# Splitting the first chunk's loads over two DMA queues, and storing the second chunk's rows earlier

## The reference, cut to what matters

```python
e = stack([tbl_f[ids[:, f]] for f in range(39)], axis=1)        # 2048 x 39 x 16
x0 = xk = e
for idx, (W, b) in enumerate([(w0, b0), (w1, b1), (w2, b2)]):
    z = relu(einsum('bhd,bkd,hks->bsd', x0, xk, W) + b[None, :, None])
    if idx != 2:
        xk = z[:, :64]          # feeds the next layer
        direct.append(z[:, 64:])
    else:
        direct.append(z)
logit = sum(concatenate(direct, axis=1), axis=-1)               # 2048 x 256
h = concatenate([logit, dense_ctx], axis=1)
y = relu(relu(h @ W_top1 + b_top1) @ W_top2 + b_top2) @ W_top3
```

## Time and profile before

| What | Number |
|---|---|
| Median of three runs | 2424.73 us |
| The profiled execution's own time | 2426.18 us |
| Its span (first to last instruction of the program) | 2424.2 us |
| TensorE (PE) busy | 2343.5 us, 97% |
| VectorE (DVE) busy | 2253.4 us, 93% |
| GpSimd (POOL) busy | 2004.7 us, 83% |
| ScalarE (ACT) busy | 1306.0 us, 54% |
| Mean granted TensorE clock | 0.994 |
| DMA | 475.43 MB, mean 196 GB/s |
| The chain that ended last | PE 94%, POOL 2%, DMA 2%, issue 1% |

### The profile page before, as it was taken

How to read it: one execution, slowest core, us unless ns; L and a number is a source line. 1 busy time by engine, 2 the same in 40 slices (tenths; PEclk the granted TensorE clock), 3 DMA queues, 4 the chain that set the end, 5 groups by cost and what they waited for, 6 DMA issues and landing times.

```text
span 2424.2 us, 32379 instructions
## 1 busy us (share of the span) xinstructions
PE 2343.5 (97%) x7936; PEld 1497.1 (62%) x7936; DVE 2253.4 (93%) x2241; ACT 1306.0 (54%) x1534; POOL 2004.7 (83%) x1284
## 2 busy tenths in 40 slices
PE   1699999999999999999999999999999999999999
PEld 0466666666666666666666666666666666666655
DVE  2699999999999999999999999999999999999973
ACT  2355555555555555555555555555555555555542
POOL 3689888988888898888889888888988888898630
PEclk9899999999999999999999999999999999999999
DMA  7878778877877887787788778778877877887710
GB/s 180 175 197 231 188 200 219 216 183 210 233 191 196 219 212 185 212 234 187 200 219 214 184 211 232 187 200 221 208 190 209 233 182 205 221 209 188 204 56 1
DMA packets 403715, 475.43 MB, mean 196 GB/s; under 512 B 171409, under 2 KB 180625, under 8 KB 403425
## 3 DMA queue, kind: packets, MB, share of 16 engines
q1 hardware_dynamic: 304354, 310.69, 52.9%
q10 hardware_dynamic: 78864, 159.39, 21.5%
q0 software_dynamic: 20480, 5.15, 1.8%
HBM read 465.41 MB, written 9.71 MB: 196 GB/s over the span
## 4 chain that ended last, share of the span: by engine, by line
PE 94%; POOL 2%; DMA 2%; issue 1%; SPq 0%; ACT 0%; DVE 0%; ACTq 0%; POOLq 0%
PE z L709 91%; POOL rows L507 1%; DMA xb<-x_rows 1%; POOL low L537 1%; DMA x_rows<-rows 1%; DMA rows<-table,index 0%; SPq L411 0%; PE x L804 0%; PE z L823 0%; PE prod_dve L804 0%; PE z L825 0%; PE z L782 0%; PE z L828 0%; PE x L805 0%; PE x L806 0%
## 5 line engine op out<-in xcount | busy, mean ns | idle before, releaser
L537 POOL TENSOR_TENSOR low<-prod_pool,high 128x1024 fp32r<-128x1024 f32 (+1 forms) x576 | 1379.9, 2396 | 220.8 <-ACT high L877 214.1
L709 PE MATMUL z<-prod_whole,w_whole 128*128 128x512 f32 (+2 forms) x2432 | 1129.4, 593 | 41.7 <-DVE prod_whole L592 41.7
L709 PE MATMUL z<-high,w_high 128*128 128x512 f32 (+1 forms) x1792 | 863.9, 482 | 31.2 <-ACT high L877 16.2
L877 ACT ACTIVATE high<-prod_pool 128x1024 fp32r<-128x1024 f32 (+1 forms) x576 | 610.9, 1061 | 405.8 <-DVE prod_pool L592 236.3
L709 PEld LDWEIGHTS z<-prod_whole,w_whole 128*128 128x128 f32 (+2 forms) x2432 | 460.9, 190 | 426.1 <-issue 364.1
L507 POOL DMA_INDIRECT rows<-table,index x640 | 613.5, 959 | 115.2 <-issue 99.7
L709 PE MATMUL z<-high,w_low 128*128 128x512 f32 (+1 forms) x1792 | 708.3, 395 | 0.0
L592 DVE TENSOR_TENSOR prod_pool<-xh,x 128x1024 f32<-128x1024 f32 x512 | 622.6, 1216 | 38.8 <-ACT x L855 33.6
L592 DVE TENSOR_TENSOR prod_whole<-xh,x 128x1024 f32<-128x1024 f32 (+1 forms) x576 | 615.7, 1096 | 7.6 <-PE z L709 1.6
L877 ACT ACTIVATE high<-prod_dve 128x1024 fp32r<-128x1024 f32 (+2 forms) x384 | 339.0, 883 | 497.0 <-DVE prod_dve L592 323.4
L709 PE MATMUL z<-low,w_high 128*128 128x512 f32 (+1 forms) x1664 | 553.5, 426 | 4.2 <-POOL low L537 4.2
(11 more groups left out here) (59 smaller groups left out, 404.6 us busy)
## 6 DMA issues: line engine op xcount, KB each, us to landing
xh<-x_rows SPq DMA_DIRECT2D x63, 2560.0 KB, 17.8
xh<-x_rows ACTq DMA_DIRECT2D x63, 2432.0 KB, 19.2
xb<-x_rows SPq DMA_DIRECT2D x128, 546.0 KB
xb<-x_rows SPq DMA_DIRECT2D x64, 468.0 KB
xa<-x_rows SPq DMA_DIRECT2D x192, 78.0 KB
rows<-table,index POOLq DMA_INDIRECT x640, 5.4
xh<-x_rows SPq DMA_DIRECT2D x65, 128.0 KB, 20.5
x_rows<-rows SPq DMA_DIRECT2D x256, 20.0 KB, 1.6
```

What stands on the lines that cost most here:

```text
L537: pool.tensor_tensor(low[0:g.rows, g.split_slot, 0:n, :], prod_pool[0:g.rows, g.slot, 0:n, :], high[0:g.rows, g.split_slot, 0:n, :].bitcas ...
L709: return pe.matmul(z[stage][:, :], weights[0:g.rows, table[stage, g.tiles[i]], :], src[0:g.rows, i, :], start=g.begins_layer and first, st ...
L877: act.activation(high[0:g.rows, g.split_slot, 0:n, :], src[0:g.rows, 0:n, :], ACT.Copy).then_inc(high_ready, 1)
```

## The change

ScalarE, ahead of `copy_xa` of chunk 0, waits until chunk 0's rows are stored and issues the pairs' third shift (`xa` and `xb`, `jj` = 2) and both parts of the odd fields; SyncE loads only the first two shifts there. SyncE stores chunk 1's rows between the first and the second part of chunk 0's even fields, and not at the beginning of chunk 1. ScalarE's `load_odd_fields(1)` moves from the beginning of `chunk(0)` to behind the second rounding of its stage 1. GpSimd issues five of chunk 2's ten gathers right behind those of chunk 1, ahead of its first low part; so 15 gathers stay in `chunk(0)`, 2, 2, 2, 2, 2, 2, 1, 1, 1 behind its nine low parts.

```diff
+GATHERED_FIRST = GATHERS // 2
...
         def load_first_fields(engine, part):
             load_fields(engine, Chunk(0, 0), part, first_fields_loaded, 0, SECOND)
+
+        def load_second_fields(engine, part):
             load_fields(engine, Chunk(0, 0), part, second_fields_loaded, SECOND, HALF_TILE)
+
+        def load_pairs(engine, c, shifts):
+            of = rows_of(c)
+            for jj in shifts:
...
+                engine.dma_start(xa[at, :], of[0:F, :]).then_inc(x0_loaded, 16)
...
+                engine.dma_start(xb[at, 0:n, :], shifted).then_inc(x0_loaded, 16)
...
             def chunk(c):
-                store_rows(c)
+                if not (c.known and c.n == 1):
+                    store_rows(c)
...
-                load_pairs(c)
+                load_pairs(sp, c, range(2 if c.known and c.n == 0 else JT))
...
                     load_first_fields(sp, 0)
+
+                    store_rows(c + 1)
+                    load_second_fields(sp, 0)
...
-                ahead = [c + 3] if not c.known or c.n + 3 < CHUNKS else []
-                if c.known and c.n == 0:
-                    ahead.insert(0, c + 2)
-                left = [(at, j) for at in ahead for j in range(GATHERS)]
+                begun = c.known and c.n == 0
+                ahead = c + 3 if not c.known or c.n + 3 < CHUNKS else None
+                left = [(ahead, j) for j in range(GATHERS if ahead else 0)]
+                if begun:
+                    left = [(c + 2, j) for j in range(GATHERED_FIRST, GATHERS)] + left
...
-            for c in range(2):
+            for c, n in enumerate((GATHERS, GATHERS, GATHERED_FIRST)):
                 make_index(Chunk(c, c))
                 begin_gather(Chunk(c, c))
-                for j in range(GATHERS):
-                    gather(c, j)
+                for j in range(n):
+                    gather(c % 2, j)
...
-                if not final:
+                during1 = {}
+                if begun:
+                    during1[1] = lambda: load_odd_fields(c + 1)
+                elif not final:
                     load_odd_fields(c + 1)
-                during1 = {}
...
             act.wait_ge(cols_loaded, 16)
+
+            act.wait_ge(stored[0], 16 * STORES)
+            load_pairs(act, Chunk(0, 0), range(2, JT))
+            load_first_fields(act, 1)
+            load_second_fields(act, 1)
             copy_xa(Chunk(0, 0))
-
-            load_first_fields(act, 1)
```

More of the change, by code:

```diff
@@ L379, in load_first_fields @@
             load_fields(engine, Chunk(0, 0), part, first_fields_loaded, 0, SECOND)
+        def load_second_fields(engine, part):
             load_fields(engine, Chunk(0, 0), part, second_fields_loaded, SECOND, HALF_TILE)
+        def load_pairs(engine, c, shifts):
+            of = rows_of(c)
+            for jj in shifts:
+                n = (SHIFTS - jj + JT - 1) // JT
+                at = slice(jj * F, (jj + 1) * F)
+                engine.dma_start(xa[at, :], of[0:F, :]).then_inc(x0_loaded, 16)
+                step = of.ap[0][0]
+                shifted = bass.AP(tensor=of.tensor, offset=of.offset + jj * step,
+                                  ap=[[step, F], [JT * step, n], [1, CN]])
+                engine.dma_start(xb[at, 0:n, :], shifted).then_inc(x0_loaded, 16)
         firsts = [g for stage in range(3) for g in PLAN[stage, 0]]
@@ L413, in store_rows @@
                                          ).then_inc(stored[c.p], 16)
[L415 to L424, removed]
             def store_feats(c):
@@ L520, in chunk @@
                 mine = [(g, at) for s, at in stages for g in groups(s, at) if g.kind == BY_POOL]
-                if ahead:
-                    make_index(ahead[0])
+                if ahead and not begun:
+                    make_index(ahead)
                 for i, (g, at) in enumerate(mine):
@@ L527, in chunk @@
                         if j == 0:
-                            if at is not ahead[0]:
+                            if begun:
                                 make_index(at)
```

## The result

The changed kernel takes 2409.72 us, the median of four runs (2408.47 to 2411.08), against 2424.69 us before (four runs): 15.0 us less, a ratio of 0.9939 with a 95% interval of 0.9923 to 0.9954. Forecast were 2412.6 us and a range of 2400 to 2421. The profiled execution took 2410.21 us for a span of 2408.4.

A forecast was written before the change was run, and what follows sets the result against it. TensorE bounds the kernel from about 134 us, so only earlier time counts: chunk 1's pairs landing 8.4 us earlier plus 3.75 us of GpSimd's gathers gave 12.1 us, hence 2412.6 us, range 2400 to 2421.

The forecast's parts named there:

- F: The landing of chunk 1's pairs, where the sum was made: 86.88 us before, forecast 78.5, 8.4 us earlier.
- Stored at 53.0: Chunk 1's rows stored at 24.6 + 1.4 + 22.7 (5.90 MB at 260 GB/s) + 4.3 = 53.0 us, against 63.31.
- the first rival: Loads up to F: the second queue brings no bandwidth, F 87.4, only 3.2 us gained, 2421.5 us; chance 0.15.
- From the stores to F, 25.5 us: From chunk 1's rows stored to its pairs landed: 23.57 + 5.5 - 3.6 = 25.5 us, ends 21 and 30.
- the 5.5 us for the even second part: On SyncE's queue ahead of chunk 1's pairs: 1.18 MB more, 5.5 us at 213 GB/s.
- The 3.6 us of SyncE's lost beginning: Behind the stores: SyncE's queue no longer loses 0.44 MB to ScalarE's fields that came first, 3.6 us saved.
- nothing by itself: Moving `load_odd_fields(1)` behind the second rounding moves the 15.0 us stall, but gains only idle time ahead of F.
- GpSimd, 3.75 us: Behind F in chunk 0: three fewer gathers of 1.25 us each, 3.75 us less, ends 0 and 4.2.
- ScalarE's issues: Four early load issues ahead of `copy_xa` of chunk 0: some 2 us in ScalarE's idle time, taken as nothing.
- the clock: Granted clock, 0.96 from 88.5 to 134 us before: no change, plus or minus 1.8 us.
- chunk 2's pairs: Landing at 111.9 us, just in time for their copy at 112.3: no cost; as rival 7.6 us late, chance 0.08.
- the slower rival: SyncE stands for chunk 1's starved gathers ahead of its stores; landing at 70 us gives 2433.9 us; chance 0.05.

The follow-up runs named there:

- the repetition: The changed kernel run again without any edit, beside three further runs on one chip: 2410.18 us.
- the run with the odd fields later still: The changed kernel with ScalarE's odd fields of chunk 1 issued behind the sixth rounding of stage 1, not the second: 2417.44 us.

## Why the prediction was right

**The sum was made at the right place.** The time goes with F and with what GpSimd adds behind it. In the runs with five early gathers and no later wait, the bound comes 42.5 to 42.9 us after F, wherever F lies between 69 and 82; the stall of 15.0 us ahead of stage 1, the largest that the change took away, was indeed idle in front of F. Undoing the part that was written for that stall didn't bring it back.

**Stored at 53.0; measured 53.16.** The size came out, the working only on the average. Counted from the first issue it is 28.4 us forecast, 29.0 measured and 28.6 in the repetition. 260 GB/s all along stood for 184 in the first ten microseconds, where the first rival was right, and 296 in the next thirteen. The two stretches of the sum were both off, and made up for each other by luck. From 24 to 50 us 6.0 MB were moved, so the 5.90 MB were through at about 50 and not at 48.7. The stores took 3.2 us from there and not 4.3, since a good part of their 64-byte pieces had gone beside those rows: 801 packets under 512 B from 45 to 50 us, 1182 from 50 to 51.

**From the stores to F, 25.5 us; measured 21.6, and 22.9 in the repetition.** This is the mis-sized term, and the main reason why the gain was 15.0 and not 12.1. Of its parts, the 5.5 us for the even second part measured 1.2 to 2.2, between the runs with and without it: 233 of its 640 rows moved from 51 to 53 us, ahead of the moment when the rows counted as stored (53.16), and that time I hadn't credited to it. The 3.6 us of SyncE's lost beginning were about right in size (25.3 less 22.9 or 21.6, 2.4 to 3.7) but put down to the wrong edit. I wrote that with the even part already flowing on the queue "this doesn't happen". It does: 175 rows against 429. What undoes it is the step that I had priced at "nothing by itself", `load_odd_fields(1)` behind the second rounding: one edit apart, the two kernels differ by those 2.4 to 3.7 us. That it works by making ScalarE's fields the second to start fits the 393 rows against 82, but isn't the whole: with a lead of 4.5 us, in the run with chunk 0's pairs on SyncE, the stretch was 25.7.

**GpSimd, 3.75 us; measured 4.4 to 4.5** (47.0 to 42.6 from F to the bound). The term held, a little past the upper end of 4.2. Issued early, the gathers cost nothing in front of F that these runs can show.

**At nothing, and nothing it was:** ScalarE's issues (24.25 to 27.0, no block), chunk 0's pairs (40.69 for 40.15), the clock (0.95 for 0.96), chunk 2's pairs (copied at 109.27 without a wait). The gathers that the slower rival wanted late had landed when SyncE issued the stores at 39.86, with both queues at work; 41.0 was forecast. But the last margin is thin, as the run with the odd fields later still shows.

## What to carry to other kernels

Where a kernel is bound by one engine after a beginning bound by loads, find the one landing from which the bound engine no longer waits, and price each edit by what it does to that landing; a long stall ahead of it may be worth nothing. With two DMA queues, look at three things, and try each, since two theories drawn from one run fell in the next: which of two transfers is issued first, whether the small pieces of one queue meet large rows on the other, and whether both run empty at about the same time. Moving 300 rows of 2 KB from one queue to the other moved this kernel by 4 us to the better (chunk 1's) or by 6 to 7 us to the worse (chunk 0's).

## What the runs showed of the hardware that was not expected

- Of two transfers issued at one moment on two queues, one can be kept back for some 5 us: 175 rows to 429 from 57 to 62 us. With an issue 1.6 us earlier the relation turned, 393 to 82. A lead of 4.5 us kept the second queue out until 69 us, and brought the first no earlier landing.
- Reading chunk 0's pairs went at 184 to 188 GB/s with one queue or two. Behind them one queue with 2 KB rows moved 102 to 105 rows in a microsecond, and two moved 100 and 98 each, 395 GB/s for 209.
- Stores in pieces of 64 bytes went at 1225 rows in a microsecond alone, and at 143, with some rows between them, beside 2 KB rows on the other queue. In 5 us of such a stretch the two queues moved 517 and 515 packets: turn by turn, whatever their size.
